# The first product's first two blocks by halves of depth, x's second half on another queue, and three matmuls on zeros fewer

## What is computed

```python
w = L0_cond_weight[itok_B_3_7]                      # [8, 1024, 1024], by the batch's id
y = einsum('bsi,boi->bso', x, w)                    # the first product
base = einsum('bth,oh->bto', y, W_up)               # the second product
logits = y @ gate_w.T + expert_bias                 # 4 experts, the best one is taken
delta = one_hot(argmax(logits)) applied to (y @ lora_A.T) @ lora_B.T
out = x + base + delta
```

## Time and profile before

| | us |
|---|---|
| median of 3 runs (lowest, highest) | 374.83 (374.81, 374.87) |
| the profiled execution, its own time | 374.81 |
| its span, first to last instruction | 373.0 |
| PE busy | 367.5 |
| DVE busy | 262.4 |
| ACT busy | 159.4 |

### The profile page before, as it was taken

How to read it: one execution, slowest core, us unless ns; L and a number is a source line. 1 busy time by engine, 2 the same in 40 slices (tenths; PEclk the granted TensorE clock), 3 DMA queues, 4 the chain that set the end, 5 groups by cost and what they waited for, 6 DMA issues and landing times.

```text
span 373.0 us, 6260 instructions
## 1 busy us (share of the span) xinstructions
PE 367.5 (99%) x2348; PEld 334.7 (90%) x2348; DVE 262.4 (70%) x519; ACT 159.4 (43%) x320; POOL 6.6 (2%) x18
## 2 busy tenths in 40 slices
PE   7999999999999999999999999999999999999996
PEld 5888888888888999889998899989999899988996
DVE  4777587696758988678755786567874777746752
ACT  5667363642527543465115651155513553144300
POOL 1000500000000000000000000000000000000000
PEclk9999999999999999999999999999999999999999
DMA  7999975871069730687026760376404861160002
GB/s 244 402 394 312 408 286 182 325 226 57 0 192 340 252 119 0 226 302 243 21 96 210 270 216 3 147 250 231 163 2 178 324 213 76 49 234 0 2 1 114
DMA packets 19598, 68.19 MB, mean 183 GB/s; under 512 B 2288, under 2 KB 2416, under 8 KB 19568
## 3 DMA queue, kind: packets, MB, share of 16 engines
q1 hardware_dynamic: 19280, 66.74, 50.0%
q10 hardware_dynamic: 288, 1.05, 0.8%
HBM read 59.39 MB, written 8.39 MB: 182 GB/s over the span
## 4 chain that ended last, share of the span: by engine, by line
PE 97%; SPq 1%; DMA 1%; DVE 0%; issue 0%; ACT 0%; DVEq 0%
PE ps_y L785 31%; PE ps_u L796 19%; PE ps_y L787 16%; PE ps_v L796 10%; PE ps_p L796 5%; PE ps_u L803 2%; PE ps_v L803 2%; PE ps_u L807 2%; PE ps_v L805 2%; PE ps_u L805 2%; PE ps_v L807 2%; PE ps_p L816 1%; DMA w_raw<-w_dram 1%; SPq L241 1%; PE ps_p L847 0%; PE ps_v L847 0%
## 5 line engine op out<-in xcount | busy, mean ns | idle before, releaser
L785 PE MATMUL ps_y<-x_hilo,w_hi 128*128 128x512 f32 x512 | 178.3, 392 | 0.3 <-DVE w_lo L510 0.3
L787 PE MATMUL ps_y<-x_hilo,w_lo 128*128 128x256 f32 x512 | 143.2, 280 | 0.0
L785 PEld LDWEIGHTS ps_y<-x_hilo,w_hi 128*128 128x128 f32 x512 | 95.8, 187 | 22.1 <-DVE w_lo L510 0.8
L787 PEld LDWEIGHTS ps_y<-x_hilo,w_lo 128*128 128x128 f32 x512 | 96.7, 189 | 0.1
L517 DVE TENSOR_TENSOR w_lo<-w_raw,w_hi 128x512 fp32r<-128x512 f32 x126 | 81.3, 688 | 16.9 <-ACT w_hi L376 16.2
L376 ACT CAST w_hi<-w_raw 128x512 fp32r<-128x512 f32 x126 | 71.8, 624 | 3.4 <-DMA w_raw<-w_dram 3.3
L391 ACT COPY small<-ps_y 128x256 f32<-128x256 f32 x64 | 23.8, 372 | 107.2 <-PE ps_y L787 107.0
L562 DVE TENSOR_TENSOR y_raw<-ps_y,small 128x256 f32<-128x256 f32 x64 | 27.2, 425 | 47.1 <-ACT small L391 47.1
L796 PE MATMUL ps_u<-up_lo,y_parts 128*128 128x256 f32 x192 | 38.4, 281 | 0.0
L796 PE MATMUL ps_u<-wide_hi,y_parts 128*128 128x256 f32 x192 | 34.8, 293 | 0.0
L573 DVE TENSOR_TENSOR y_parts<-y_raw,y_parts 128x512 fp32r<-128x512 f32 x50 | 32.5, 687 | 1.3 <-ACT y_parts L394 0.9
(11 more groups left out here) (108 smaller groups left out, 393.7 us busy)
## 6 DMA issues: line engine op xcount, KB each, us to landing
w_raw<-w_dram SPq DMA_DIRECT2D x64, 512.0 KB, 4.4
rows<-x_dram SPq DMA_DIRECT2D x16, 512.0 KB, 5.7
out_dram<-rows SPq DMA_DIRECT2D x15, 512.0 KB, 2.6
x_raw<-xT_dram SPq DMA_DIRECT2D x14, 512.0 KB, 5.0
up_raw<-w_up_dram SPq DMA_DIRECT2D x8, 512.0 KB, 12.4
wide_stage<-w_up_dram SPq DMA_DIRECT2D x4, 512.0 KB, 14.0
thin_stage<-w_up_dram SPq DMA_DIRECT2D x4, 512.0 KB, 9.4
x_raw<-xT_dram ACTq DMA_DIRECT2D x2, 512.0 KB, 4.2
```

What stands on the lines that cost most here:

```text
L785: pe.matmul(ps_y[c % 2][:, :], w_hi[:, n % RING, cols], x_hilo[:, :, k, :], start=(k == 0), stop=False)
L787: last = pe.matmul(ps_y[c % 2][:, S:2 * S], w_lo[:, n % RAWS, cols], x_hilo[:, 0, k, :], start=False, stop=(k == KC - 1))
```

## The change

It does five things. `WARM` is 15 for 18. In batch 0, PE runs depth steps 0 to 3 of block 0, then 0 to 3 of block 1 (into the other bank), then 4 to 7 of block 0 and of block 1; all other blocks run whole. ACT asks for x's first half only, and after DVE's memset of `warm_f`. SP asks for x's second half, behind W blocks 0 and 1 and ahead of block 2. ACT and DVE split x's first two quarters, all of W block 0, W block 1, then x's last two quarters, then block 2.

```diff
--- before.py
+++ after.py
@@ -55,7 +55,7 @@
     PARTS = 7
     SUMS = 5
     STEPS = 9
-    WARM = 18
+    WARM = 15
     BLOCKS = B * OC
     assert T == 2 and 4 * ER == P and HALF == 512 and B >= 4 and 2 * GL <= P
 
@@ -297,7 +297,9 @@
                 return i
 
             i = adapter(0)
-            i = load_blocks(0, 4, i)
+            i = load_blocks(0, 2, i)
+            sp.dma_start(x_raw[:, 1, XS:KC, :], xT[0, :, XS:KC, :]).then_inc(x_raw_in[1], 16)
+            i = load_blocks(2, 4, i)
             for n in range(4, OC):
                 load_unit(n - 4)
                 i = load_blocks(n, n + 1, i)
@@ -477,18 +479,17 @@
                 for n in splits_after(b):
                     w_hi_part(n)
 
-            for d in range(XD):
-                ks = slice(d * XS, (d + 1) * XS)
-                act.dma_start(x_raw[:, 1, ks, :], xT[0, :, ks, :]).then_inc(x_raw_in[d], 16)
-            for q in range(XQ - 1):
+
+            act.wait_ge(warm_step, 1)
+            act.dma_start(x_raw[:, 1, 0:XS, :], xT[0, :, 0:XS, :]).then_inc(x_raw_in[0], 16)
+            for q in range(XQ // XD):
                 x_hi(0, q)
-            for q in range(QUARTERS // 2):
+            for q in range(QUARTERS):
                 first_w_hi(q)
-            x_hi(0, XQ - 1)
-            for q in range(QUARTERS // 2, QUARTERS):
-                first_w_hi(q)
-            for n in range(1, AHEAD):
-                w_hi_part(n)
+            w_hi_part(1)
+            for q in range(XQ // XD, XQ):
+                x_hi(0, q)
+            w_hi_part(2)
             for b in range(B):
                 first_product(b)
                 if b < PLAIN:
@@ -743,15 +744,14 @@
             dve.memset(warm_f[:, :], 0.0).then_inc(warm_step, 1)
             dve.wait_ge(warm_step, 1)
             dve.tensor_copy(warm[:, :], warm_f[:, :]).then_inc(warm_ready, 1)
-            for q in range(XQ - 1):
+            for q in range(XQ // XD):
                 x_lo(0, q)
-            for q in range(QUARTERS // 2):
+            for q in range(QUARTERS):
                 first_w_lo(q)
-            x_lo(0, XQ - 1)
-            for q in range(QUARTERS // 2, QUARTERS):
-                first_w_lo(q)
-            for n in range(1, AHEAD):
-                w_lo_part(n)
+            w_lo_part(1)
+            for q in range(XQ // XD, XQ):
+                x_lo(0, q)
+            w_lo_part(2)
             for b in range(B):
                 first_product(b)
                 if b < PLAIN:
@@ -766,27 +766,37 @@
                 for _ in range(WARM):
                     pe.matmul(ps_y[0][:, :], warm[:, 0:P], warm[:, :], start=True, stop=True)
 
+            def steps(b, c, ks):
+                n = b * OC + c
+                for k in ks:
+                    if n == 0 and k % QK == 0:
+                        pe.wait_ge(w_ready, k // QK + 1)
+                    elif k % HK == 0:
+                        pe.wait_ge(w_ready, n * QUARTERS + (k // HK + 1) * (QUARTERS // HALVES))
+                    if c == 0 and k % XK == 0:
+                        pe.wait_ge(x_ready, b * XQ + k // XK + 1)
+                    cols = slice(k * P, (k + 1) * P)
+                    pe.matmul(ps_y[c % 2][:, :], w_hi[:, n % RING, cols], x_hilo[:, :, k, :],
+                              start=(k == 0), stop=False)
+                    last = pe.matmul(ps_y[c % 2][:, S:2 * S], w_lo[:, n % RAWS, cols], x_hilo[:, 0, k, :],
+                                     start=False, stop=(k == KC - 1))
+                if k == KC - 1:
+                    last.then_inc(block_done, 1)
+
             def first_product(b):
-                for c in range(OC):
+                if b == 0:
+
+                    for ks in (range(XS), range(XS, KC)):
+                        for c in range(2):
+                            steps(0, c, ks)
+                for c in range(2 if b == 0 else 0, OC):
                     n = b * OC + c
                     if n >= 2:
                         pe.wait_ge(y_full_ready, n - 1)
                     if c == 1 and b > PLAIN:
 
                         pe.wait_ge(row_step, rows_before[b] - 3)
-                    for k in range(KC):
-                        if n == 0 and k % QK == 0:
-                            pe.wait_ge(w_ready, k // QK + 1)
-                        elif k % HK == 0:
-                            pe.wait_ge(w_ready, n * QUARTERS + (k // HK + 1) * (QUARTERS // HALVES))
-                        if c == 0 and k % XK == 0:
-                            pe.wait_ge(x_ready, b * XQ + k // XK + 1)
-                        cols = slice(k * P, (k + 1) * P)
-                        pe.matmul(ps_y[c % 2][:, :], w_hi[:, n % RING, cols], x_hilo[:, :, k, :],
-                                  start=(k == 0), stop=False)
-                        last = pe.matmul(ps_y[c % 2][:, S:2 * S], w_lo[:, n % RAWS, cols], x_hilo[:, 0, k, :],
-                                         start=False, stop=(k == KC - 1))
-                    last.then_inc(block_done, 1)
+                    steps(b, c, range(KC))
 
             def quarter_wide(ps, p, q, k, start, stop, gated):
                 for y, up, more in ((0, up_hi, 2 * GL), (0, None, 0), (1, up_hi, GL)):
```

## The result

The change makes the kernel 0.3% slower: 375.86 us against 374.86 us in the median of eight executions each, ratio 1.003 with a 95% interval of 1.0017 to 1.0042. The forecast was 376.6 us. The two profiled executions took 375.64 and 374.81 us, their spans are 373.6 and 373.0 us. Two executions of all, one of the kernel before (607.19 us) and one of experiment 6 (518.86 us), ran at a mean granted clock of 0.56 and 0.66 and are left out of every comparison.

What follows compares the result with a forecast made beforehand. PE is busy almost throughout, so block 2's start moves the end one for one. New waits of 0.78 and 1.08 us put block 2's second step 1.80 us later: 374.81 + 1.80 = 376.6 us, range 374.0 to 377.4 (own range 375.6 to 377.0).

Steps and rivals of the forecast that it cites:

- Two of the signs by which the prediction called itself wrong: Wrong if x lands before about 10.8, W block 0 is issued well before 4.25, or steps after waits are 0.64 apart.
- 15 matmuls on zeros: PE's start: three fewer end at about 7.42 us instead of 8.11, worth nothing since the product starts at 8.45 anyway.
- x's first half: ACT's load, issued at 1.40 instead of 0.74 us: lands at 5.20 instead of 4.54, hidden under W's landing.
- PE starts at 8.45: First product: W block 0, issued at 4.25, lands at 7.51 as before; gain between 0 and 0.16 us, taken as 0.
- rival 2: SP's read of the ids shortens, W's issue comes 1.2 us earlier, loads 1.28 us apart: 373.8 us; chance 0.15.
- an early start with the spacing of before: W issued early but loads spaced as before: ends at +0.5 us, called no change.
- The other doubt: W block 0 might land sooner without x's second half beside it; the most allowed makes the sum below 376.4 us.
- Block 1 after half of block 0: PE asks for block 1 after four steps, at 9.96 us; ready at 10.74: a new wait of 0.78 us.
- x's second half: Third on SP's queue, lands at 11.87 us; PE goes on at 13.33: second new wait of 1.08 us.
- The wait for `y_full` before block 2: PE's wait at 14.35 us before block 2 goes away: 0.23 us with its slower first step.
- The sum: Second step of block 2 at 16.60 us against 14.80: +1.80 us, giving 376.6 us.
- Rival 3: PE's idle gaps drop the array to 1.2 GHz: 1.5 us more, 378.1 us, not shown by the page; chance 0.07.

Runs made afterwards that it cites:

- experiment 6: The changed kernel with x's second half loaded behind one W block, split before W block 1, and PE's blocks whole; 376.18 us, ratio 1.0035.
- experiment 5: The changed kernel with 18 matmuls on zeros again instead of 15; 376.30 us, ratio 1.0035.
- experiment 9: The kernel before with only PE's order of the change, halves of blocks 0 and 1; 375.79 us, ratio 1.0035.
- experiment 3: The changed kernel with PE running blocks 0 and 1 whole, as before; 378.64 us, ratio 1.0101.
- experiment 7: The changed kernel with W blocks 0 and 1 also loaded and split by halves of depth; 376.52 us, ratio 1.0043.
- 8: The changed kernel with W blocks 0 and 1 loaded by halves and x's first half issued without waiting for DVE's memset; 377.03 us, ratio 1.0056.
- experiment 2: The changed kernel without ACT's wait on DVE's memset, so x's first half is issued at 0.74 us; 376.25 us, ratio 1.0041.
- experiment 1: The kernel before with ACT issuing both halves of x only after DVE's memset; 375.52 us, ratio 1.002.
- 4: The changed kernel with x's second half issued by ACT directly behind its first, not by SP; 376.10 us, ratio 1.004.
- experiment 10: The kernel before with ACT issuing both halves of x behind GpSimd's first memset, near 1.0 us; 375.21 us, ratio 1.001.
- 11: The kernel before with W block 0 loaded by two DMAs of half its depth; 375.67 us, ratio 1.0024.
- 12: The kernel before with x issued near 1.0 us and W block 0 loaded by halves; 375.14 us, ratio 1.001.

## Why the prediction was right, and where its steps were not

The sign held, and so did the reason at large: PE gets its data later, in two new waits, and has nothing to make it up with. The size is little more than half of the forecast one: 1.0 us for 1.8. Two of the signs by which the prediction called itself wrong came true: W block 0 was issued well before 4.25 us, and x's second half landed before 10.8. That the median lies in the forecast's own range (375.6 to 377.0) is in part luck. The stretch that the prediction worked out lost 0.53 us in the trace, which alone gives 374.81 + 0.53 = 375.3; the rest came from outside it. Point by point:

- **15 matmuls on zeros.** Worth nothing: in the profile they end near 7.3 (7.42 forecast). What I had wrong is that 8.11, the end of the 18, is a fixed time. In experiments 5 and 9 the last zeros started at 8.8 and 8.5 and the product stood right behind them (9.01 and 8.70); nor do 15 always end near 7.3: in 3, 6, 7 and 8 the last of them started at 7.7 to 8.0.
- **x's first half.** Forecast 5.20, landed 5.6. It took 4.2 us instead of 3.8, and stayed hidden as forecast, under W block 0's 6.9.
- **W block 0.** This is the step that failed: "PE starts at 8.45". I held its issue at 4.25 us; it was 2.73, since the read of the ids shortened, and all four loads came earlier than in the sum. That was the first half of rival 2. Its second half, loads 1.28 us apart, did not come true: W block 0 took 4.1 us from its issue, W block 1 came 2.0 us after it (6.9 to 8.9) and x 1.75 after that. The price that I put on just this case, an early start with the spacing of before, was +0.5 us (by the prediction's own terms it is +0.6: 1.80 less the 1.2 of the earlier issue); the trace has +0.53. I gave that case no chance of its own. The other doubt, that W block 0 would land sooner without x's second half beside it, did not come true: in experiment 2 that half was issued behind it and only x's first half ahead of it, and it took 3.4 us from its issue, not less than 3.26.
- **Block 1 after half of block 0.** Forecast: a wait of 0.78 us ending at 10.74. The rows have 0.77 us ending at 10.43 in the change, and 0.78 us in experiment 9, which undid everything else. The step is shown. Its size is a little more than that: a row counts from the modelled end of the last matmul, the sum from 1.51 us for four steps. Counted like the sum, the wait is 10.43 - 9.49 = 0.94 us, since the four steps began 0.47 us earlier and W block 1 only landed 0.4 us earlier.
- **x's second half.** From issue to landing 6.9 us (6.5 forecast); with the earlier issue 10.6 instead of 11.9. From the landing to PE 1.5 us, as the sum had it (1.46). The wait was therefore 0.2 us and not 1.08: the largest error of the sum. Experiment 2, where the issue is late again, has it at 0.87 us ending at 12.66.
- **What is gone.** The wait for `y_full` before block 2 is gone, as forecast, and nothing waits after it.
- **The sum.** 0.47 us earlier at the start; waits of 0.94 and 0.21 us; a slow first step after each, 0.10 and 0.07; less the old wait at block 2 with its slow step, 0.25, and 0.07 for steps that ran at 0.347 us instead of 0.353: -0.47 + 0.94 + 0.21 + 0.17 - 0.25 - 0.07 = +0.53 us in the trace, where I had +1.80.

**Which part costs.** In these nine traces one load sets the start of block 2, by how late it lands and by how many steps PE still has to do when it goes on with it:

| run | the load | landed | PE goes on at | steps left | second step of block 2 |
|---|---|---|---|---|---|
| before | W block 0 | 7.5 | 8.45 | 16 | 14.80 |
| the change | x's second half | 10.6 | 12.14 | 8 | 15.33 |
| 1 | W block 0 | 8.2 | 9.14 | 16 | 15.19 |
| 2 | x's second half | 11.1 | 12.66 | 8 | 15.90 |
| 3 | x's second half | 11.2 | 12.69 | 12 | 18.87 |
| 4 | W block 1 | 9.6 | 11.17 | 12 | 15.87 |
| 6 | x's second half | 9.5 | 10.98 | 12 | 15.65 |
| 9 | W block 1 | 9.5 | 11.04 | 12 | 15.73 |
| 10 | W block 1 | 10.1 | 11.71 | 8 | 15.00 |

In each row the last column is, within 0.1 us, the time at which PE goes on, plus 0.35 us for each step left and one more, plus 0.1 for the slow first one (3 has 1.45 for the fall of the clock on top, and the kernel before 0.25 for its wait for `y_full` and the slow step behind it). So it is not the last of the four loads that counts: in 4 and 9 all four are in by 9.6, a microsecond before the change's, and the time is no better. Two things cost in the change. The halves let PE ask for W block 1 with twelve steps left instead of eight; by this sum that alone would put the second step of block 2 at 10.43 + 13 x 0.35 + 0.1 = 15.1 (an estimate), 0.3 us late in spite of the earlier start. x's place behind two W blocks makes it 15.33. With whole blocks (3) that place costs 3.8 us in the median, as twelve steps are left instead of eight and the clock falls in most executions; the halves take most of that back. Where all of x stays on ACT's queue (1, 4) W block 0 gets late instead (8.2 and 8.3).

That the start of block 2 moves the end one for one is borne out. In the traces of the change and of all twelve experiments the execution is longer than that of before by as much as block 2's second step is late, within 0.1 us, plus 0.3 us where the slower steps of the last section are found. Only the change and 6 have another 0.2 us, and that lies outside their spans.

**The reading of the ids.** With both halves of x issued by ACT from 0.74 us on (before, 9, 11) the second read took 1.96 to 1.99 us, with only the first half (2, 8) 1.68 and 1.23, with x at 0.98 (10, 12) 1.14 and 1.12, and with x at 1.44 (the change, 1, 3 to 7) 0.46 to 0.50, however the other loads were ordered. Experiments 1 and 2 turn it on and off by that one line, in one trace each. That x's issue sets it is shown. Two windows, of before and of the change (last columns: DMA share and GB/s), say when x's packets start to move:

```profile
1.60:1.80 0.20, 0.00 (x0) 0.00 (x0) 0.20 (x1) 0.17 (x1) 0.11 (x1) 1.00 0.53 102
```

```profile
2.00:2.40 0.40, 0.40 (x1) 0.40 (x2) 0.00 (x0) 0.40 (x1) 0.32 (x5) 1.00 0.00 0
```

No other load has been asked for by then. Before, they move beside nearly the whole read (1.59 to 3.58). In the change none moves before 2.4, when the read (1.60 to 2.06) is over; ACT's issuing (1.44 to 1.81) does lie beside that read and does not lengthen it. So what is left is the packets; no run tests them apart from the issue.

**The clock.** Rival 3 happens in some executions: one of the eight of the change took 377.69 us with a mean granted clock of 0.995, the mark of the execution of experiment 3 whose trace shows the fall; it was not traced itself. Experiments 4, 6 and 8 had one such execution each; of the 61 executions of before in the three groups that the comparisons use, none was below 0.998. The fall does not explain every long execution: 377.14 (5), 377.05 (6) and 377.15 us (9) show 1.000. I wrote that the page would not show a fall; it does, as a granted clock of 0.50. What it does not show is the low level at the start: in the kernel before the granted clock reads 1.00 from 2 to 5 us, while the matmuls on zeros are 0.43 us apart. The Trainium skill, page "TensorE: Matmul & The Clock Gate", section "HAM oscillation — how this bites in real kernels", says that an idle gap can put the array back to half rate; experiment 3's 3.21 us did, and the change's three gaps of 0.2 to 0.8 us did not in the execution that was traced.

**What stays open.** The profiled pair is 0.83 us apart, the medians 1.0. The spread of the change's executions (375.64 to 376.16, without the one above) is not traced; the slower steps of the last section would add 0.3 us to some, if they occur there. What delays the early loads (the slow patch of the earlier trace rows) is not found. Two landings in a row that are 2.0 us or more apart stand in the traces of most orders, but not in 1 and 4, where ACT asks for both halves of x from 1.44 us on and the loads behind them land at most 1.7 us apart. A load's semaphore counts up in 16 steps, and their times in the traces say how part of it looks: in the kernel before the first and the last step are 0.3 us apart for W block 0, 0.8 for block 1 and 1.7 for block 2, in experiment 1 0.7 to 0.8 for every load. So some sixteenths of the loads fall behind the others; why is open. Whether the delay goes by the byte isn't settled either: half of W block 0 took 4.5 us from its issue in experiment 7, but 2.7 and 2.8 in 8 and 11.

## What to carry to other kernels

At a kernel's start, list the loads that must be in before the main engine can run without a gap, and for each add up its landing, its preparation, and the work that the engine still has to do behind the point at which it asks for it; the largest of these sums sets the time, not the last landing. A finer order of the work lets the engine start earlier, but it also asks for the next operand with more work left behind it. Before moving a DMA, look at what else touches memory beside it: here one issue moved by 0.7 us took 1.5 us off another engine's small read. And where you put an idle time at nothing because something else covers it, see in more than one execution whether that cover is there.

## What was not expected of the hardware

- A small read of DRAM by SP took 1.99 us beside x's moving packets and 0.46 us ahead of them.
- The matmuls on zeros went from 1.2 to 2.4 GHz at very different times from execution to execution: the last of 18 started at 7.7 us in the profile of before, at 8.5 in experiment 9 and at 8.8 in experiment 5; in experiment 10 at 7.4.
- The first product's steps have two paces in batch 0. After its restart at block 2 the kernel before runs at 0.347 us a step; so do the change and experiments 1, 5, 7 and 11. The other eight (2, 3, 4, 6, 8, 9, 10, 12) stay at 0.353 to the end of the batch. Over the 48 steps from block 2 on that is 0.3 us, and part of what they lose. The first and the last of five starts in a row of experiment 2, and of the change:

```profile
25.79 0.40 PE L778 MATMUL ps_y<-x_hilo,w_hi 128*128 128x512 f32 x1
...
27.20 0.40 PE L778 MATMUL ps_y<-x_hilo,w_hi 128*128 128x512 f32 x1
```

```profile
25.73 0.39 PE L779 MATMUL ps_y<-x_hilo,w_hi 128*128 128x512 f32 x1
...
27.12 0.39 PE L779 MATMUL ps_y<-x_hilo,w_hi 128*128 128x512 f32 x1
```

1.41 us for four steps against 1.39. What chooses between them is not known.
